# Cross-attention and a feed-forward layer on one core: tiles turned by a trip through DRAM and one block transpose on VectorE

## What is computed

```python
def attention(x, context, Wq, Wk, Wv, Wout, bout):        # 8 heads of 128
    qh, kh, vh = split(x @ Wq), split(context @ Wk), split(context @ Wv)
    # batch is folded into the rows: every row sees all J = 2*77 = 154 keys
    sim = einsum('hid,hjd->hij', qh, kh) * 128 ** -0.5
    mean = sim.mean(-1, keepdims=True)
    attn = softmax((sim - mean) * 1.5 + mean)
    return merge(einsum('hij,hjd->hid', attn, vh)) @ Wout + bout

def ffn(x, W_r, W_k, W_v, mu_r, mu_k):
    x_prev = shift_rows_by_one(x)                          # zero at each batch's start
    xr = mu_r * x + (1 - mu_r) * x_prev
    xk = mu_k * x + (1 - mu_k) * x_prev
    return sigmoid(xr @ W_r.T) * (square(relu(xk @ W_k.T)) @ W_v.T)

x = x + attention(layernorm(x), ctx_768, ...)              # x: 2 x 2048 x 512, float32
x = x + ffn(layernorm(x), ...)                             # ctx_768: 2 x 77 x 384
```

## Time and profile before

| | |
|---|---|
| median of 3 runs | 828.47 us (828.04 to 829.88) |
| profiled execution, span from first to last instruction | 830.5 us |
| profiled execution's own time | not recorded apart from its span |
| busy: TensorE, VectorE, ScalarE, GpSimd | 792.1, 688.1, 465.8, 295.0 us |
| mean granted TensorE clock | 0.989 |
| DMA | 27.85 MB, 34 GB/s over the span |

### The profile page before, as it was taken

How to read it: one execution, slowest core, us unless ns; L and a number is a source line. 1 busy time by engine, 2 the same in 40 slices (tenths; PEclk the granted TensorE clock), 3 DMA queues, 4 the chain that set the end, 5 groups by cost and what they waited for, 6 DMA issues and landing times.

```text
span 830.5 us, 14007 instructions
## 1 busy us (share of the span) xinstructions
PE 792.1 (95%) x4243; PEld 690.7 (83%) x4243; DVE 688.1 (83%) x1767; ACT 465.8 (56%) x1542; POOL 295.0 (36%) x524
## 2 busy tenths in 40 slices
PE   7999999899999999999999999999999999999988
PEld 6978788798978788797979888797878879797867
DVE  6877688988898889888898898889888898889662
ACT  2675665465656555564646555555655646464631
POOL 2001244353414334352424435341434435241441
PEclk9999899999999999999999999999999999999998
DMA  9420000001010000101010000101000000100000
GB/s 314 154 81 34 14 14 13 27 13 38 14 39 13 25 25 0 38 13 38 13 38 13 13 26 12 38 13 38 13 25 25 7 30 13 38 1 26 1 25 26
DMA packets 16821, 27.85 MB, mean 34 GB/s; under 512 B 2302, under 2 KB 5656, under 8 KB 16793
## 3 DMA queue, kind: packets, MB, share of 16 engines
q1 hardware_dynamic: 16793, 27.51, 10.0%
HBM read 19.12 MB, written 8.39 MB: 33 GB/s over the span
## 4 chain that ended last, share of the span: by engine, by line
PE 43%; DVE 33%; ACT 11%; issue 8%; POOL 3%; DVEq 0%; DMA 0%; ACTq 0%; POOLq 0%; SPq 0%
DVE xn2T L795 11%; DVE xT L795 10%; PE turn L342 5%; PE turn L344 5%; PE turn L343 5%; ACT probs L633 4%; PE scores L343 4%; PE scores L344 4%; PE scores L342 4%; PE attended L344 4%; PE attended L343 4%; PE attended L342 4%; DVE neg_max L824 2%; DVE gate L855 2%; DVE act_lo L749 2%
## 5 line engine op out<-in xcount | busy, mean ns | idle before, releaser
L795 DVE STREAM_TRANSPOSE xn2T<-normed 32x128 f32<-32x128 f32 x512 | 154.8, 302 | 8.4
L795 DVE STREAM_TRANSPOSE xT<-normed 32x128 f32<-32x128 f32 x480 | 145.0, 302 | 6.2
L625 ACT ACTIVATE probs<-scores,neg_max 128x154 f32<-128x154 f32 x256 | 97.3, 403 | 81.6 <-DVE neg_max L824 81.6
L342 PE MATMUL scores<-A_hi,xT_hi 128*128 128x462 f32 (+1 forms) x384 | 137.0, 357 | 0.1
L343 PE MATMUL scores<-A_lo,xT_hi 128*128 128x462 f32 (+1 forms) x384 | 135.0, 352 | 0.0
L344 PE MATMUL scores<-A_hi,xT_lo 128*128 128x462 f32 (+1 forms) x384 | 134.6, 351 | 0.0
L633 ACT ACTIVATE probs<-probs,inv_sum 128x154 f32<-128x154 f32 x256 | 84.3, 419 | 65.7 <-DVE inv_sum L829 65.7
L342 PE MATMUL attended<-B_hi,pT_hi 128*128 128x512 f32 x288 | 113.1, 393 | 1.8 <-DVE pT_lo L749 1.8
L344 PE MATMUL attended<-B_hi,pT_lo 128*128 128x512 f32 x288 | 113.1, 393 | 0.0
L343 PE MATMUL attended<-B_lo,pT_hi 128*128 128x512 f32 x288 | 113.0, 393 | 0.0
L1003 POOL TENSOR_SCALAR mix_now<-xn2T,mu_k_cols 128x128 f32<-128x128 f32 x128 | 46.0, 380 | 181.7 <-DVE xn2T L795 181.6
(11 more groups left out here) (178 smaller groups left out, 1792.1 us busy)
## 6 DMA issues: line engine op xcount, KB each, us to landing
x_in<-in_x SPq DMA_DIRECT2D x32, 256.0 KB, 2.6
out<-x SPq DMA_DIRECT2D x32, 256.0 KB, 2.0
wq<-in_L_xattn_Wq SPq DMA_DIRECT2D x4, 512.0 KB, 9.0
wout<-in_L_xattn_Wout SPq DMA_DIRECT2D x1, 2048.0 KB
wv<-in_L_xattn_Wv SPq DMA_DIRECT2D x1, 1536.0 KB, 11.1
wk<-in_L_xattn_Wk SPq DMA_DIRECT2D x2, 576.0 KB, 5.6
raw_wk<-in_L_ffn_W_k SPq DMA_DIRECT2D x1, 1024.0 KB, 8.3
raw_wr<-in_L_ffn_W_r SPq DMA_DIRECT2D x1, 1024.0 KB, 5.2
```

What stands on the lines that cost most here:

```text
L342: te.matmul(psum, left[0], right[0], start=first, stop=False)
L625: last = nc.scalar.activation(probs[:, h * J:(h + 1) * J], S[b][:, (h - h0) * J:(h - h0 + 1) * J], ACT.Exp, bias=neg_max[:, h:h + 1], accu ...
L795: last = v.transpose(dst[32 * q:32 * q + 32, :, 32 * i:32 * i + 32], blocks[32 * i:32 * i + 32, :, q, :])
```

## The change

- **Probabilities** are no longer turned by TensorE. They are laid out in four quarters of 352 columns (two heads of 154 keys, 20 columns of high parts, a one, again 20 and a one, padding), stored to DRAM as rows (`store_probs`), and read back by four DMAs (`hand_probs`), one for each quarter of columns, so that quarter q lies on the partitions 32q to 32q+31. Then a single VectorE block transpose over all 128 partitions (`turn_blocks`, 128 x 1408) gives `pT`. High and low parts are taken from SBUF.
- **x and x2** go the same way (`hand_x`, `hand_x2`: one store, a wait for it, four loads with runs of 512 bytes into the one tile `handed`), then one transpose of 128 x 512. Tiles 0 and 1 of x are turned by TensorE.
- **Order**: each TensorE step begins with scores(t+1); VectorE's step ends with the turn and the split of the probabilities of tile t+1; ScalarE's step likewise.
- **Norms** move from VectorE to ScalarE (`x_norm`, `x2_norm`, with a shift that GpSimd computes as a third small instruction). Normalising the probabilities moves from ScalarE (nine instructions) to VectorE (one, 1232 columns). The mixes work on pairs: VectorE makes `delta` = x - x_prev and xr, GpSimd xk. The output's second half moves to GpSimd, with the factor 0.5 folded into W_v.
- **Start**: scores(0) comes before the values; B is made in 16 pieces of (head, 128 keys), copied to `staged`, stored to DRAM and loaded again in the new order of rows; all loads of B must have landed before its first split.
- **Buffers**: `normed` and `handed` are one tile each, shared by x and x2; `delta` lies on `gate`, so `differences(q)` waits for the outputs of pair q-1.

The diff, cut:

```diff
@@ sync
+            def hand_x(t):
+                sp.wait_ge(xn_ready, t + 1)
+                sp.dma_start(x_dram[bass.ds(t * P, P), :], normed[:]).then_inc(xn_stored, 16)
+                sp.wait_ge(xn_stored, 16 * (t - 1))
+                if begun(t - 3):
+                    sp.wait_ge(xn2T_ready, t - 2)
+                rows = x_dram[bass.ds(t * P, P), :].rearrange("(r i) (q k) -> q i r k", i=Q, q=4)
+                for q in range(4):
+                    sp.dma_start(handed[q * Q:(q + 1) * Q, :].rearrange("i (r k) -> i r k", r=4), rows[q]
+                                 ).then_inc(xn_handed, 16)
+            def store_probs(t):
+                sp.wait_ge(probs_ready, t + 1)
+                sp.dma_start(p_dram[bass.ds(t * P, P), :], probs[:].rearrange("p q k -> p (q k)")
+                             ).then_inc(probs_stored, 16)
+            def hand_probs(t):
+                sp.wait_ge(probs_stored, 16 * (t + 1))
+                if begun(t - 1):
+                    sp.wait_ge(probs_turned, t)
+                rows = p_dram[bass.ds(t * P, P), :].rearrange("(r i) (q k) -> q i r k", i=Q, q=4)
+                for q in range(4):
+                    sp.dma_start(probs_handed[q * Q:(q + 1) * Q, :, :], rows[q]).then_inc(probs_landed, 16)
             def step(g, s):
+                if half == 0 and is_pair(q - 1):
+                    store(q - 1, 0, s)
+                    store(q - 1, 1, (s + 1) % 4)
+                if is_tile(t + 2):
+                    hand_x(t + 2)
+                if is_tile(t + 1):
+                    store_probs(t + 1)
                 if is_tile(t + 4) and is_tile(t):
                     sp.wait_ge(x2_ready, t + 1)
                     sp.dma_start(x_in[s][:], xt[bass.ds((t + 4) * P, P), :]).then_inc(x_loaded[s], 16)
+                if is_tile(t + 1):
+                    hand_probs(t + 1)
+                if is_tile(t):
+                    hand_x2(t)
@@ tensor
             def step(g, s):
-                if is_tile(t):
-                    turn_probs(t, q, half)
                 if is_tile(t + 1):
                     scores(t + 1)
@@ scalar, step after
+                squares_hi(q)                       # odd steps
+                x_norm(t + 2, (s + 2) % 4)
+                exponentials(t + 1, 0)
+                mixed_high("r", q)                  # even steps
+                exponentials(t + 1, 1); exponentials(t + 1, 2)
+                mixed_high("k", q)                  # even steps
+                pack_hi(t + 1)
+                x_hi(t + 2)
+                open_gate(q, half)
+                x2_norm(t, s)
+                rectify(q, 0)                       # even steps
+                probs_hi(t + 1, 0); probs_hi(t + 1, 1); probs_hi(t + 1, 2)
+                rectify(q, 1)                       # even steps
@@ vector
+            def turn_blocks(dst, src, width):
+                blocks = "p (r k i) -> p r k i"
+                return v.transpose(dst.rearrange("p k (r i) -> p r k i", i=Q),
+                                   src.rearrange(blocks, r=4, k=width, i=Q))
+            # step after
+                x_statistics(t + 2, (s + 2) % 4, g + (s + 2) // 4 + 1)
+                open_values(q - 1, 1)               # even steps
+                x2_turn(t - 1, 1 - half, q if half == 0 else q + 1)
+                maxima(t + 1, 0)
+                differences(q); mix_r(q)            # even steps
+                maxima(t + 1, 1); maxima(t + 1, 2)
+                mixed_low("r", q)                   # even steps
+                squares_lo(q)                       # odd steps
+                normalise(t + 1)
+                x_turn(t + 2)
+                pack_lo(t + 1)
+                x_lo(t + 2)
+                mixed_low("k", q)                   # even steps
+                add_x(t, g, s)
+                open_values(q, 0)                   # odd steps
+                probs_turn(t + 1)
+                probs_lo(t + 1, 0); probs_lo(t + 1, 1); probs_lo(t + 1, 2)
@@ gpsimd, step after
+                x_root(t + 2)
+                output(q - 1, 1, (s + 1) % 4)       # even steps
+                mix_k(q); keep_halo(q, ...)         # even steps
+                x2_root(t)
+                squares(q)                          # even steps
+                output(q, 0, (s - 3) % 4)           # odd steps
```

More of the change, by code:

```diff
@@ L24 @@
 P = 128
+Q = 32
 HEADS = 8
@@ L186, in xattn_ffn @@
         S = [bank(f"scores{i}") for i in range(3)]
-        T = [bank(f"turn{i}") for i in range(3)]
+        T = [bank(f"ffn{i}") for i in range(3)]
         O = bank("attended")
-        XB = bank("turned_x")
+        XB = bank("spare")
         def sem(name):
@@ new lines, in exponentials @@
+            def exponentials(t, b):
+                h0, h1 = HEAD_BANKS[b]
+                if b == 0:
+                    if begun(t - 1):
+                        act_e.wait_ge(probs_stored, 16 * t)
+                act_e.wait_ge(max_ready, 3 * t + b + 1)
+                for h in range(h0, h1):
+                    q, cols = head_columns(h)
+                    last = nc.scalar.activation(probs[:, q, cols], S[b][:, (h - h0) * J:(h - h0 + 1) * J],
+                                                ACT.Exp, bias=neg_max[:, h:h + 1], accum_out=row_sum[:, h:h + 1])
+                if h1 == HEADS:
+                    last.then_inc(exp_done, 1)
@@ L686, in step @@
-                if not is_pair(q):
-                    weights_hi(2 * t + 1)
+                    exponentials(t + 1, 0)
+                if is_pair(q) and half == 0:
+                    mixed_high("r", q)
+                if is_tile(t + 1):
+                    exponentials(t + 1, 1)
+                    exponentials(t + 1, 2)
+                if is_pair(q) and half == 0:
+                    mixed_high("k", q)
+                if not is_pair(q) and t == 0:
+                    for i in range(4):
+                        act_e.wait_ge(B_stored[i], 64)
+                    for i in range(8):
+                        weights_hi(i)
+                        values_hi(i)
+                    for i in range(8, BLOCKS):
+                        values_hi(i)
@@ L693, in _ @@
+                if is_tile(t + 1):
+                    for i in range(3):
+                        probs_hi(t + 1, i)
+                if is_pair(q) and half == 0:
+                    rectify(q, 1)
             act_e.wait_ge(ctxT_keys_ready, 1)
@@ L875, in step @@
+                if is_tile(t + 1):
+                    maxima(t + 1, 0)
+                if is_pair(q) and half == 0:
+                    differences(q)
+                    mix_r(q)
+                if is_tile(t + 1):
+                    maxima(t + 1, 1)
+                    maxima(t + 1, 2)
+                if is_pair(q) and half == 0:
+                    mixed_low("r", q)
                 if is_pair(q) and half == 1:
                     squares_lo(q)
+                if not is_pair(q) and t == 0:
+                    for i in range(4):
+                        dve.wait_ge(B_stored[i], 64)
+                    for i in range(8):
+                        weights_lo(i)
+                        if i % 2 == 0:
+                            values_lo(i)
+                    values_lo(8)
+                    pack_values()
@@ L909, in step @@
-                if is_tile(t) and half == 1 and not last:
-                    x2_turn(t, half, q + 1, range(1, 4) if is_pair(q) else range(4))
+                if is_pair(q) and half == 1:
+                    open_values(q, 0)
+                if is_tile(t + 1):
+                    probs_turn(t + 1)
+                    for i in range(3):
+                        probs_lo(t + 1, i)
             ctx_view = XB[:, 0:CC * J].rearrange("p (c j) -> p c j", j=J)
@@ L1005, in mix @@
[L1005 to L1008 removed]
+                    last = gp.tensor_scalar(mixed["k"][:, c, :], delta[:, c, :], mu["k"][:, c:c + 1], 1.0,
+                                            ALU.mult, ALU.mult)
+                last.then_inc(k_scaled, 1)
+                pool.wait_ge(k_scaled, q + 1)
@@ new lines, in squares, with output, values_lo @@
+            def squares(q):
+                for j in range(2):
+                    pool.wait_ge(relu_ready, 2 * q + j + 1)
+                    a = act[:, 2 * j:2 * j + 2, :]
+                    gp.tensor_tensor(a, a, a, ALU.mult).then_inc(square_ready, 1)
+            def output(q, j, slot):
+                pool.wait_ge(gated, 2 * q + j + 1)
+                gp.tensor_tensor(x2[slot][:], gate[j][:], x2[slot][:], ALU.add).then_inc(out_ready, 1)
+            def values_lo(c):
+                pool.wait_ge(B_hi_ready, c + 1)
+                gp.tensor_tensor(B_lo[:, c, :], B_rows[:, c, :], B_hi[:, c, :].bitcast(F32), ALU.subtract
+                                 ).then_inc(B_odd_ready, 1)
```

904 lines of the change are left out of this document (454 added, 450 removed).

## The result

| | before | after |
|---|---|---|
| median of the runs | 828.37 us (828.04 to 829.88) | 898.83 us (896.49 to 899.76) |
| ratio, 95% interval | | 1.0842 [1.0823, 1.0861] |
| profiled span | 830.5 us | 894.7 us |
| mean granted TensorE clock | 0.989 | 0.932 |

What follows compares the result with a forecast made beforehand. VectorE's in-order loop through the probabilities' DRAM trip, 48.1 us a pair, was taken to bound the kernel, not TensorE. 133.5 + 15 x 25.2 + 14 x 22.9 + 36.6 = 868.7 us span, 866.7 median (4.6% slower), range 798 to 918.

Steps and rivals of the forecast that it cites:

- the even step's work: VectorE's even step up to the packed probabilities: 12.6 us; with trip, turn and split, a step of 25.2 us.
- R: The probabilities' trip through DRAM, store to landed loads: 8.65 us, bounds 7.3 and 11.8.
- the start: Start-up until tile 2's attention is over: 133.5 us, against 118.1 in the kernel before.
- the end: From tile 31's attention to the output's store: 36.6 us, against 34.6 in the kernel before.
- The lower price: VectorE's full-height block transposes: 0.70 us for 128x512, 1.64 for the probabilities; the upper price was 1.26 and 3.5.
- the rival at 952: Full-height transposes on VectorE at the upper price, 85 us more over 29 steps: 952 us; chance 0.08.
- L: The time of a tile's last low part of the probabilities on VectorE, from which each step's loop is added up.
- The odd step: VectorE's odd step: 10.3 us to the packed probabilities, 22.9 with trip, turn and split.
- The loop: The 29 steps from tile 2's attention to tile 31's: 15 of 25.2 us and 14 of 22.9.
- TensorE-bound at 800: Rival: the loop closes in less than 21.8 us a step and TensorE is the bound: 800 us; chance 0.22.
- Trips that slow each other: Rival: DRAM trips slow each other, R at 11.8, 91 us more over 29 steps: 957 us; chance 0.12.
- The sign: Slower or faster: faster if the loop averages 22.7 us a step instead of 24.1; slower given 0.74, faster 0.24.

Runs made afterwards that it cites:

- double_load: Changed kernel with the probabilities' four quarters loaded twice by SP, VectorE waiting for both loads; 1063.79 us (one run).
- no_trip: Changed kernel without the DRAM stores and loads that turn normed x, normed x2 and probabilities; VectorE turns what lies in SBUF; 828.70 us.
- short_add: Changed kernel with GpSimd's addition that completes xk cut from 1024 columns to 4; 887.1 us, 1.0671 of before.
- no_trip_filled: no_trip with nine added matmuls, results overwritten, before TensorE's wait for xk's low part in even steps; 825.54 us.
- reorder: Changed kernel with x loaded behind the probabilities and x2, and maxima, exponentials and packing ahead of the mixes on VectorE and ScalarE; 869.82 us.
- late_both: Changed kernel with the probabilities' turn and split moved to the next step, behind the first maxima, and x2's turn behind that split; 876.80 us.

## Why the prediction was right, and where its sizes were off

**The mechanism held.** The pace is set by VectorE's order and the trip: of 5.3 us more of trip 5.1 came out in each step (double_load), taking the trips out gave 70 us (no_trip). TensorE isn't the bound, though it is still the busiest. But the loss, 70 us, is nearly twice the 38 that were forecast: the sizes that missed by most (the even step's work, R, the start, the end) were all too small.

**Full-height transposes**: 1.645 us and 0.708 measured for 1.64 and 0.70 forecast. The lower price, chosen because it also explained the 0.302 of the earlier trace rows, was right; the rival at 952 falls. Normalising 1.44 (1.45).

**`differences` waits for GpSimd's output**: it started 3.72 after L (427.97 to 431.69), forecast 3.6, and the wait is on the row.

**The odd step**: 22.86 us, forecast 22.9; its turn of x stood for x's trip to 9.05 after L (9.25). The terms of that 9.25 (3.6, 2.0, 1.35, 2.2) add up to 9.15.

**The even step**: 26.5 us, forecast 25.2. The packing's 12.6 became 13.4, R's 8.65 became 9.3, and turn and split took 3.8 (3.95). Ahead of the packing the mix of xr took 2.34 (1.7), so the exponentials were over at 10.3 and not 9.6, and the low part of xr took 2.63 (1.2). The prediction had priced the low part as if VectorE were alone, and GpSimd's addition held it (short_add): without the addition the packing comes 0.7 us earlier in the mean.

**The trip R**: 9.3 and 9.15 us, 9.1 in the mean of the loop, forecast 8.65. The store landed in 3.2 (3.4), the issue behind it came as forecast (3.68 after the store's, with SP's wait and the x load: 3.95), but the four quarters needed 5.5 from the first issue to the turn (4.7; its own terms give 4.6, since 2.0 and 2.2 are 4.2 and not 4.3, so the forecast was 3 us of loop too high there). Their 128 loads landed 3.5 us after issue in the median. The price had been chosen because the DMA engines "would be under half busy"; they were, 39% over a pair, but 84% while the quarters were on their way (window 445.20 to 450.70, 226 GB/s). The Trainium skill's sum for one DMA (DMA: Bandwidth & Descriptors, Anatomy of one DMA) would make it 2.4 for 176 KB by itself, and R 7.9, as an estimate; its fit is for DMAs that GpSimd issues, and these are issued by SP. The measurement decides, and it is 1.3 us above that sum and 0.6 above mine.

**The loop**: 712.7 us, forecast 698.6. In the mean of tiles 5 to 27 even steps took 26.8 us and odd ones 22.5, against 25.2 and 22.9: 18 us more for 15 and 14 of them, of which the first and the last steps took 4 back.

**The start**: tile 2's attention over at 140.0, forecast 133.5. The 6.5 us were lost ahead of the turn of probs(0), which began at 72.75, forecast 66.4 for its landing. SP's queue:

```profile
59.04 0.36 SPq L382 DMA_DIRECT2D prob_rows<-probs  x1
59.45 2.82 SPq L352 DMA_DIRECT2D value_rows<-staged  x4
62.31 0.65 SPq L361 DMA_DIRECT2D B_rows<-value_rows  x1
...
64.52 1.75 SPq L391 DMA_DIRECT2D probs_handed<-prob_rows  x4
```

The four stores of `staged` held the queue for 2.8 us (two issues of 0.43 and two of 0.92, where I had counted 0.45 for each), and with five loads of B they stand between the store of probs(0) and its loads, 5.5 us apart. These loads then landed 5.2 to 6.9 us after issue, where the loop's took 3.5 in the median, and the turn came 8.2 us behind the first of them. From there on the forecast's distances held: the turns of probs(0), (1) and (2) came 6.3, 5.6 and 5.7 us late.

**The end**: 42.0 us, forecast 36.6, and 39.8 to 44.1 in every kernel with the new order, with trips or without. The granted clock there is 0.83 (window 860 to 894), with TensorE busy 20 of 34 us; the forecast had it at full speed. Counted from the end of tile 31's attention, xr's low part was done at 17.7 (15.5), again behind the mix and GpSimd's addition, and the gate, behind an idle of 9.7 us, ran its twelve matmuls at half clock, 0.43 us each and 5.3 in all (2.8), so that the keys ended at 28.9 and not 23.9. These are 5.0 of the 5.4 us.

**The sum**: 6.5 (start), 14.1 (loop) and 5.4 (end) are the 26.0 us between the forecast span of 868.7 and 894.7. The median lies 4.1 above that span, and the forecast took 2.0 off. That term was wrong: every execution with a recorded time and span took 1.7 to 2.1 us more than its own span (the profiled one of the changed kernel 896.49 and 894.7). The two spans are of one execution each, some 4 us longer than the median one before and 2.3 us shorter than it after.

**The rivals.** TensorE-bound at 800 falls by no_trip too: even with R at nothing its loop is 659 and not 632, since keys wait 1.75 us a pair for xk's low part (24 of the 27 us are left in no_trip_filled, 656 us, where the clock doesn't fall). That rival's price had taken the trip for TensorE's only obstacle; the low parts of the mixes are a second one. Trips that slow each other by 3.1 us each (957) fall: R is 0.6 above its forecast. The sign hung on 1.4 us a step; that far below the forecast no kernel with the trips came (reorder: 23.7 us a step; 22.7 was the turning point).

## What to carry to other kernels

When an in-order engine must wait for something that its own earlier instruction set off, add up that loop by itself, from its start to the next one's start, before looking at who is busiest: here the busiest engine lost work and the kernel lost 8%. Moving such a wait shows the next one behind it (x2's trip, then scores, then the mixes), so price all of them before hiding one. Look also at what GpSimd does beside each instruction of that loop: its addition held one instruction of VectorE here, and the reordering put a dearer one in its place. Look at what stands in the issuing queue between a store and its load: one unrelated load with a wait of its own was worth 20 us, and it ate the whole of another improvement.

## What the runs showed of the hardware that was not expected

- TensorE's granted clock fell to half (1.2 of 2.4 GHz) behind an idle of only 1.75 us, but not behind every such idle: all 13 pairs of no_trip have one of 1.6 to 1.8 us before the keys, and five were 1.5 us longer; in late_both it was four of 13. After 3.75 us idle in the changed kernel the slices showed 0.75, 0.50 and 0.90.
- A subtraction of 128x1024 on VectorE with both inputs in SBUF took 2.65 us beside GpSimd's addition of the same width and 1.22 alone. It ended 1.08 us after the addition in all 16 cases. In reorder, where VectorE's normalising began first, the addition took 3.18 us and not 2.17, and an instruction of 128x80 behind it on VectorE took 1.65 us and not 0.24.
- At the start four stores out of `staged` held SP's queue for 2.8 us, two with issues of 0.43 us and two of 0.92; the issues in the loop took 0.35 to 0.46.
- Four loads of 176 KB, issued 0.46 apart, landed in 3.5 us each in the median; the DMA engines were busy 39% of the pair, but 84% during these loads.
